# The second attention's row maxima: mask added on VectorE, a compact inverse, and values carried into the next block

## What is computed

```python
qkv = (layernorm(x) @ attn_w.T + attn_b).reshape(b, n, 16, 24).transpose(0, 2, 1, 3)
q, k, v = jnp.split(qkv, 3, axis=-1)
mask = jnp.arange(n)[:, None] <= jnp.arange(n)[None, :]
scores = jnp.where(mask, einsum('bhki,bhqi->bhkq', k, q) / sqrt(8), -10000.0)
probs = softmax(scores, axis=2)
out = einsum('bhkq,bhkl->bhql', probs, v) ...
x = x + out @ out_w.T + out_b
```

## Time and profile before

| | |
|---|---|
| median of 3 runs | 783.54 us (780.2 to 790.93) |
| profiled execution | 791.89 us, span 790.0 us, mean granted TensorE clock 0.945 |
| attention b | 343 to 601 us of the span, about |
| its first scores of block 0 | 318 to 343 us |
| PE, DVE, ACT, POOL busy | 703.7, 507.1, 454.5, 432.1 us |

### The profile page before, as it was taken

How to read it: one execution, slowest core, us unless ns; L and a number is a source line. 1 busy time by engine, 2 the same in 40 slices (tenths; PEclk the granted TensorE clock), 3 DMA queues, 4 the chain that set the end, 5 groups by cost and what they waited for, 6 DMA issues and landing times.

```text
span 790.0 us, 14471 instructions
## 1 busy us (share of the span) xinstructions
PE 703.7 (89%) x4962; PEld 490.7 (62%) x4962; DVE 507.1 (64%) x965; ACT 454.5 (58%) x801; POOL 432.1 (55%) x444
## 2 busy tenths in 40 slices
PE   4888995799999999989999889898878899999996
PEld 2455554577777776765555555555546677778784
DVE  6678884657665575566477777776566666755520
ACT  2768774465566655456456556556464455566563
POOL 4455341477778775343244444444443777777773
PEclk9999997899999999999599999999678999999998
DMA  5110410000000005504355545544102000000000
GB/s 177 38 37 19 67 19 2 1 1 0 1 0 0 1 1 187 187 2 138 133 174 176 188 147 199 176 149 135 56 27 80 1 15 14 0 13 14 14 14 27
DMA packets 30726, 51.98 MB, mean 66 GB/s; under 512 B 2256, under 2 KB 7376, under 8 KB 30672
## 3 DMA queue, kind: packets, MB, share of 16 engines
q1 hardware_dynamic: 30480, 51.01, 20.6%
q10 hardware_dynamic: 192, 0.26, 0.1%
HBM read 26.88 MB, written 24.12 MB: 65 GB/s over the span
## 4 chain that ended last, share of the span: by engine, by line
PE 49%; POOL 14%; issue 14%; DVE 11%; ACT 9%; ACTq 1%; POOLq 1%; DVEq 0%; DMA 0%
PE banks L220 45%; POOL f_h_lo L1121 5%; POOL f_g_lo L1128 5%; ACT b_prob L1439 4%; PE banks L212 2%; DVE a_mx L644 2%; POOL b_prob L1636 2%; DVE xn L182 2%; ACT a_prob L547 1%; DVE a_prob L656 1%; DVE a_straight L629 1%; ACT xn L198 1%; DVE f_hidden L1071 1%; PE banks L956 1%; DVE f_gate L1067 1%
## 5 line engine op out<-in xcount | busy, mean ns | idle before, releaser
L1128 POOL TENSOR_TENSOR f_g_lo<-f_gelu,f_g_hi 128x512 fp32r<-128x512 f32 x128 | 168.2, 1318 | 67.4 <-ACT f_g_hi L1023 67.0
L1022 ACT ACTIVATE f_gelu<-banks,cols 128x512 f32<-128x512 f32 x128 | 88.3, 690 | 140.1 <-PE banks L220 139.2
L1636 POOL TENSOR_SCALAR_AFFINE_SELECT b_prob<-b_prob 128x512 f32<-128x512 f32 x128 | 82.3, 646 | 120.2 <-ACT b_prob L1439 119.8
L220 PE MATMUL banks<-f_g_hi,whi 128*128 128x512 f32 x320 | 133.3, 416 | 15.1 <-POOL f_g_lo L1128 15.1
L1523 DVE TENSOR_REDUCE b_segment_max<-banks 128x6 f32<-128x768 f32 x128 | 115.9, 947 | 41.7 <-PE banks L220 41.7
L1439 ACT ACTIVATE b_prob<-banks 128x768 f32<-128x768 f32 x128 | 102.6, 810 | 64.9 <-PE banks L220 58.4
L220 PE MATMUL banks<-f_g_lo,whi 128*128 128x512 f32 x320 | 128.1, 400 | 0.0
L1121 POOL TENSOR_TENSOR f_h_lo<-f_hidden,f_h_hi 128x512 fp32r<-128x512 f32 x60 | 77.7, 1295 | 59.1 <-DVE f_h_hi L1074 59.1
L220 PE MATMUL banks<-f_h_hi,whi 128*128 128x512 f32 x256 | 104.4, 408 | 3.0 <-POOL f_h_lo L1121 2.5
L220 PE MATMUL banks<-f_h_lo,whi 128*128 128x512 f32 x256 | 102.1, 399 | 0.0
L1023 ACT ACTIVATE f_g_hi<-banks,cols 128x512 fp32r<-128x512 f32 x128 | 87.2, 681 | 0.0
(11 more groups left out here) (124 smaller groups left out, 1092.7 us busy)
## 6 DMA issues: line engine op xcount, KB each, us to landing
f_h_hi<-b_q_dram SPq DMA_DIRECT2D x16, 512.0 KB, 4.1
f_h_lo<-b_k_dram SPq DMA_DIRECT2D x16, 512.0 KB, 5.1
b_o_dram<-b_o SPq DMA_DIRECT2D x8, 1024.0 KB, 4.4
b_q_dram<-b_q_hi SPq DMA_DIRECT2D x16, 256.0 KB, 3.1
b_k_dram<-b_k_hi SPq DMA_DIRECT2D x16, 256.0 KB, 3.0
w_stage<-in_wF SPq DMA_DIRECT2D x8, 352.0 KB, 3.2
b_q_dram<-b_q_lo SPq DMA_DIRECT2D x8, 256.0 KB, 3.0
b_k_dram<-b_k_lo SPq DMA_DIRECT2D x8, 256.0 KB, 3.1
```

The costliest lines, as they stand in the source:

```text
L220: return nc.tensor.matmul(out, lhsT, rhs, start=start, stop=stop)
L1022: nc.scalar.activation(gf[c % 2][:, :], z_bank[c % 2], ACT.Gelu, scale=scale).then_inc(s_gf, 1)
L1128: nc.gpsimd.tensor_tensor(lo[:, c, :], gf[c % 2][:, :], hi[:, c, :].bitcast(F32), ALU.subtract).then_inc(s_glo[c % 2], 1)
L1636: nc.gpsimd.affine_select(out=pr, in_=pr, compare_op=ALU.is_ge, fill=0.0, base=0, pattern=[[0, 4], [1, P]], channel_multiplier=-1).then_in ...
```

## The change

1. `pe_first` has no mask products. Per head it makes one product of 256 columns and one of 128, and waits for all reductions of the step before.
2. `dve_first` runs, per head and query tile, one instruction that adds the mask (0 or -1e30, a zero tile for the middle third) to the scores, writes the sum as bf16 to a tile that nothing reads, and takes the maximum into the tile to be transposed. `dve_max` and its copies are gone.
3. The denominators are loaded once each as 128 x 64 and inverted by one instruction behind step 2; SP stores the inverse to DRAM and loads it repeated. POOL waits for that load.
4. The values and the output copy of step 7 move into step 0 of the next block.

```diff
 def pe_first(pe, m, n):
-                for p in range(PAIRS):
-                    wait(pe, s_red, UNITS * m.t + PAIRS * n + p - 1)
-                    for j in (2 * p, 2 * p + 1):
-                        out = first_pass[:, j, 0:3 * P].rearrange("p (c k) -> p c k", c=3)
-                        mm(out[:, 0:3:2, :], ident_b[:, :], mask[:, 0:2, :], start=True, stop=False)
-                for c, (qt, kt) in enumerate(((0, 0), (1, 0), (1, 1))):
+                wait(pe, s_red, UNITS * m.t + PAIRS * n)
+                for qt, into in ((1, slice(P, 3 * P)), (0, slice(0, P))):
                     for j in range(GROUPS):
-                        last = mm(first_pass[:, j, c * P:(c + 1) * P], q[rows_of(j), g, at + qt * P:at + (qt + 1) * P],
-                                  k[rows_of(j), g, at + kt * P:at + (kt + 1) * P], start=False, stop=c == 2)
+                        last = mm(first_pass[:, j, into], q[rows_of(j), g, at + qt * P:at + (qt + 1) * P],
+                                  k[rows_of(j), g, at:at + (qt + 1) * P])
                 last.then_inc(s_p1, 1)
...
 def dve_first(dve, m, n):
                 dve.wait_ge(s_p1, STEPS * m.t + n + 1)
+                if n % HALF == 0:
+                    wait(dve, s_mt, HALVES * (m.t - 1) + n // HALF + 1)
+                dve.sem_inc(s_turn_max, 1)
                 for p in range(PAIRS):
-                    nc.vector.reduce_max(seg[:, g, s, 2 * p:2 * p + 2, :],
-                                         first_pass[:, 2 * p:2 * p + 2, 0:3 * P].rearrange("p b (c k) -> p b c k", c=3),
-                                         AX.X).then_inc(s_red, 1)
+                    for j in (2 * p, 2 * p + 1):
+                        for qt, into in ((0, slice(0, P)), (1, slice(P, 3 * P))):
+                            last = nc.vector.tensor_tensor_reduce(
+                                out=masked[:, j, into], in0=first_pass[:, j, into], in1=mask_row[:, into], scale=1.0,
+                                scalar=MASKED, op0=ALU.add, op1=ALU.max,
+                                accum_out=mx[g // PAIRS][:, s, qt, j, g % PAIRS:g % PAIRS + 1])
+                    last.then_inc(s_red, 1)
...
-            def dve_inverse(dve, b, half):
-
-                if half == 0:
-                    dve.wait_ge(s_ol, 32 * (b.t + 1))
-                at = slice(half * T, (half + 1) * T)
-                nc.vector.reciprocal(inv[:, at], den[:, at]).then_inc(s_inv, 1)
+            def dve_inverse(dve, b):
+
+                dve.wait_ge(s_ol, 32 * (b.t + 1))
+                nc.vector.reciprocal(den_inv[:, :], den[:, :]).then_inc(s_inv, 1)
...
 pool_normalise:
-                pool.wait_ge(s_inv, HALVES * (b.t + 1))
+                pool.wait_ge(s_ol, 32 * (b.t + 1))
+                pool.wait_ge(s_il, 16 * (b.t + 1))
...
 sp_out:
-                sp.dma_start(den[:, :], view[:, DB:REP, :]).then_inc(s_ol, 16)
+                sp.dma_start(den[:, :], view[:, DB, :].rearrange("h (c t) -> h c t", t=DEN_COLS)).then_inc(s_ol, 16)
+                sp.wait_ge(s_inv, v["read"])
+                sp.dma_start(inv_dram.ap().rearrange("h (c t) -> h c t", t=DEN_COLS), den_inv[:, :]).then_inc(s_is, 16)
+                sp.wait_ge(s_is, v["stored"])
+                sp.dma_start(inv[:, :], inv_dram.ap().unsqueeze(1).to_broadcast([HB, DB, TOK])).then_inc(s_il, 16)
...
 pe_step:
                 if n:
                     pe_values(pe, b, n - 1)
+                elif before:
+                    pe_values(pe, b.after(-1), STEPS - 1)
...
 act_body:
+                    if before and n == 0:
+                        act_out(act, b.after(-1), GROUPS - 1)
...
 dve_body:
-                    if before and n in (OUT_AT - 2, OUT_AT - 1):
-                        dve_inverse(dve, b.after(-1), n - (OUT_AT - 2))
+                    if before and n == INVERSE_AT:
+                        dve_inverse(dve, b.after(-1))
```

More of the change, by code:

```diff
@@ L262, in build @@
         o_dram = nc.dram_tensor("b_o_dram", (GROUPS, P, TOK), F32)
+        inv_dram = nc.dram_tensor("b_inv_dram", (HB, TOK), F32)
         s_wB = sem("b_weights_loaded")
@@ L279, in pool_b_constants @@
                                     base=0, pattern=[[-1, P]], channel_multiplier=1).then_inc(s_cp, 1)
-            nc.gpsimd.affine_select(out=mask[:, :, :], in_=mask[:, :, :], compare_op=ALU.is_ge, fill=MASKED,
-                                    base=0, pattern=[[0, GROUPS], [-1, P]], channel_multiplier=1).then_inc(s_cp, 1)
+            nc.gpsimd.affine_select(out=mask[:, 0:3:2, :], in_=mask[:, 0:3:2, :], compare_op=ALU.is_ge, fill=MASKED,
+                                    base=0, pattern=[[0, 2], [-1, P]], channel_multiplier=1).then_inc(s_cp, 1)
         def sp_b_constants(sp):
@@ L1174, in attention_b @@
             split = {k: sb(f"b_{k}", [P, TOK], F32R) for k in ("q_hi", "q_lo", "k_hi", "k_lo")}
-            seg = sb("b_segment_max", [P, GROUPS, SEQS, GROUPS, 3])
+            masked = sb("b_masked_scores", [P, GROUPS, 3 * P], BF16)
+            mask_row = mask[:, 0:3, :].rearrange("p c k -> p (c k)")
             mx = [sb(f"b_max{i}", [P, SEQS, 2, GROUPS, PAIRS]) for i in range(HALVES)]
@@ L1179, in attention_b @@
             oT = sb("b_oT", [P, TOK])
-            den = sb("b_den", [P, TOK])
+            DEN_COLS = HB * TOK // P
+            den = sb("b_den", [P, DEN_COLS])
+            den_inv = sb("b_den_inv", [P, DEN_COLS])
             inv = sb("b_inv", [P, TOK])
@@ L1198, in attention_b @@
             s_red = sem("b_segments_reduced")
-            s_mx = sem("b_max_ready")
+            s_turn_max = sem("b_max_turn")
             s_mt = sem("b_max_transposed")
@@ L1211, in attention_b @@
             s_ol = sem("b_output_loaded")
+            s_is = sem("b_inverse_stored")
+            s_il = sem("b_inverse_loaded")
             s_on = sem("b_output_normalised")
@@ L1219, in attention_b @@
             MAX1_AT, T_AT, Q_AT, K_AT, V_AT, MAX0_AT, OUT_AT = 0, 1, 2, 3, 4, 5, 6
+            INVERSE_AT = 2
             GATE_AT = {2: 0, 4: 1, 6: 2}
@@ L1367, in pe_body @@
                     pe_step(pe, b, n, before, one, two, parts)
-                pe_values(pe, b, STEPS - 1)
+                if not one:
+                    pe_values(pe, b, STEPS - 1)
             def pe_front(pe, b, at, c):
@@ L1483, in act_body @@
                         nxt["act_tanh"](act, FIRST_BLOCK, GATE_AT[n], HEAD_PAIR)
-                act_out(act, b, GROUPS - 1)
                 if not one:
+                    act_out(act, b, GROUPS - 1)
                     nxt["act_tanh"](act, FIRST_BLOCK, KC - 1, HEAD_PAIR)
@@ L1568, in dve_body @@
                         norm.dve_apply(dve, n2, False)
-                    if one and n == MAX0_AT - 1:
-                        dve_max(dve, n1, 0)
                     if one and not two and n == OUT_AT:
@@ L1624, in dve_tail @@
                 if c == KC - 1:
-                    dve_inverse(dve, LAST_BLOCK, 0)
-                    dve_inverse(dve, LAST_BLOCK, 1)
+                    dve_inverse(dve, LAST_BLOCK)
                 if c == KC:
```

13 lines of the change are left out of this document (1 added, 12 removed).

## The result

| | before | after |
|---|---|---|
| median of 4 runs | 785.21 us (780.2 to 790.93) | 811.15 us (808.86 to 813.05) |
| profiled execution, span | 791.89, 790.0 us | 809.59, 807.6 us |
| attention b, first exponential of block 0 to that of block 7 | 223.2 us | 246.5 us |

The ratio is 1.033 (95% interval 1.025 to 1.041): slower, and outside the predicted 765 to 806. (Ratios here compare undisturbed executions only, so a median over all of a kernel's runs can lie a little above its ratio.)

A forecast was written before the change was run, and what follows sets the result against it. It took PE and ACT's exponential as a matched pair bounding the attention's half step, with PE leading overall; -12 us at equal clock and +13 from a falling clock gave +1, so 785 us, range 765 to 806.

The forecast's parts named there:

- What bounds the kernel: Attention half step with first scores: PE's issue and ACT's exponential level at about 1.45 us, so removing masks gains little.
- D = 2.2 us, reads free: VectorE's eight mask-and-maximum instructions per step take 2.2 us together, with accumulator reads hidden; the other end was 3.3.
- Rival 2: VectorE becomes the bound: D = 3.3, 804 to 806 us, chance 0.14; middle case D = 2.6, 790, chance 0.10.
- Carried values, -1.1 a block: At block turns, moving step 7's values later brings the next scores 1.6 us sooner, costing 0.5: net -1.1.
- Inverse, -1.0 + 0.5: Per block, POOL's stall for the reciprocal goes, -1.0 us; VectorE's new wait for late denominators costs PE 0.5.
- Equal clock, -1.4 a steady block: Sum for a steady attention block at unchanged clock: -0.2 + 0.4 - 1.1 - 1.0 + 0.5 = -1.4 us.
- Feed-forward, -1: Eight of 64 steps lie in the feed-forward before the attention; they gain 1 us in all.
- The clock falls in every block: Attention without 128-row mask products: granted clock well under 0.92 in blocks 0 to 6, five of eight steps low.
- The price, 0.6 us a low step: Attention step at 1.2 GHz without masks takes 4.2 us against 3.6: 21 us in all, less 8 already lost, +13.
- Rival 3: Attention clock stays down for whole blocks: +14 us, 798 to 803, chance 0.12.
- Rival 4: SP's wait for the inverse's store makes rows late for first scores: 1.5 us a block, 794, chance 0.08.
- rival C: Raised after the experiments, no chance given: PE's idle time in each step, not the rows used, lowers the clock.

The follow-up runs named there:

- e6: Kernel before with only the carried values added: 774.13 us, ratio 0.988 to before.
- e4: Kernel before with the carried values and the compact inverse, without the new maxima: 767.91 us, ratio 0.978 to before.
- e9: Changed kernel with four unused 128-row mask products per step put where PE waits for the exponential: 780.51 us, ratio 0.993 to before.
- e13: e9 with the inverse behind step 3 instead of step 2: 782.11 us, ratio 0.997 to before.
- e14: e4 with the inverse behind step 3 instead of step 2: 781.65 us, ratio 0.995 to before.
- e1: Changed kernel with the four 128-row mask products of each step issued again behind the wait for the maxima, result unused: 786.65 us, ratio 1.003 to before.
- e8: Changed kernel with the values of heads 0 and 1 moved ahead of the second pair's scores: 775.93 us, ratio 0.989 to before.
- e2: e1 with each unused mask product on 32 rows of the array instead of 128: 802.85 us, ratio 1.019 to before.
- e15: e13 with VectorE's blocks 1 to 6 written out instead of looped: 784.03 us, ratio 0.994 to before.
- e7: e1 with two unused mask products per step instead of four: 808.59 us, ratio 1.034 to before.

## Why the prediction was wrong, step by step

- **What bounds the kernel: right.** From the first exponential of a step to the second, on ScalarE, it takes 1.34 or 1.35 us at full clock in before (blocks 2 to 5) and as much in after (steps 4 to 6); at the low level 1.59 or 1.60 in after. PE waits where it issued masks:

```profile
500.67 0.45 PE L220 MATMUL banks<-f_h_hi,f_h_lo 32*128 32x256 f32 x4 [0.87 <-ACT b_prob L1445]
```

- **D = 2.2 us, reads free: right.** DVE in after (start, length), one step's first three of eight:

```profile
500.62 0.28 DVE L1536 CUSTOM_DVE_ANT_0 b_masked_scores<-banks,b_mask 128x128 bf16<-128x128 f32 x1
500.82 0.08 DVE L1536 DVE_READ_ACCUMULATOR2_ANT b_max<- 128x1 f32 x1
500.82 0.42 DVE L1536 CUSTOM_DVE_ANT_0 b_masked_scores<-banks,b_mask 128x256 bf16<-128x256 f32 x1
501.17 0.08 DVE L1536 DVE_READ_ACCUMULATOR2_ANT b_max<- 128x1 f32 x1
501.17 0.28 DVE L1536 CUSTOM_DVE_ANT_0 b_masked_scores<-banks,b_mask 128x128 bf16<-128x128 f32 x1
...
502.84 0.08 DVE L1536 DVE_READ_ACCUMULATOR2_ANT b_max<- 128x1 f32 x1
```

  0.20 to 0.21 and 0.35 us start to start, 2.22 for the eight, each read at the next one's start. Rival 2, both cases, is out, and the chosen end was the right one.
- **Carried values, -1.1 a block: right.** e6's blocks 3 to 5 take 29.3 us on average, before's three quiet ones 30.25: -1.0.
- **Inverse, -1.0 + 0.5: right in sum.** e4's blocks 3 to 5 take 28.8: -0.5. POOL's product no longer waits (510.08 in after, no releaser). The new wait for the denominators is there: in after only in block 6 (1.78 us; 2.13 in e9), where steps are short, but in e4, at full clock, in each of blocks 1 to 6, with 0.57 to 2.12 us.
- **Equal clock, -1.4 a steady block: right.** e9's blocks 2, 4 and 5 take 28.8 against 30.25: -1.4. The same blocks of e4 take 28.8 too, so in a steady block the new maxima are worth nothing, where I had +0.2.
- **Feed-forward, -1: not contradicted.** The attention starts at 342.4 against 344.7 in the profiled pair, and at 341.0 to 345.7 in the other kernels.
- **The clock falls in every block: right.** I said five of eight steps of 4.2 us in seven blocks, 147 us low. Blocks 0 to 6 of after have 2 x (1 - clock) x length = 18 + 22 + 27 + 18 + 17 + 26 + 22 = 150 us.
- **The price, 0.6 us a low step: wrong, and this is the step that failed.** Blocks 1 to 5 of after average 35.7 us with 22.1 low, against 28.9 at full clock: 6.8 / 22.1 = 0.31 us for each low one. Step by step: the 18 steps of blocks 1 to 6 of after that lie wholly at the low level take 4.83 us on average, and the same steps at full clock (e9, one of them from e4) 3.46, so each costs 1.4. The prediction had this rate on its own page (a loss of 0.33 us for each low one, from 110 products in 14 us) and used it for the time lost before; for the time after it took 5.3 - 1.08 = 4.2, as if the masks' 1.08 us at 1.2 GHz came back in full. They lie in part in the exponential's shadow at the low level too, by the argument that the prediction itself made for full clock: 0.7 comes back in the half step shown above and nothing in step 1 (4.75 us with and without). The 5.3 itself, with masks, was about right for the four wholly low steps of before (4.58 to 6.06 us, 5.36 on average); with q in it such a step is longer (6.08 in block 1 before, 5.67 after).

With the rate: blocks 0 to 6 have 150 us low against 36 (6 + 18 + 3 + 8), 115 x 0.31 = +36. My -7 and -1.7 at equal clock beside it make +27; measured +23.3. On the whole, -12 + 36 = +24 on the median, 809 for 811 measured. The 0.31 is taken from five of these seven blocks, so this sum shows that the terms fit together and tests little; with the prediction's own 0.33 it would be 38 for the 36. Rival 3, whole blocks low, is out as a mechanism, because clock 0.64 to 0.75 means half to three quarters of a block; its price was too small for the same reason. Rival 4 didn't happen in after (F never waits for a load there), but e13 and e14 show that it was a single step away.

## What to carry to other kernels

Ask of work that is to be removed what it covers and what it keeps up: where PE waits for another engine anyway, a product removed there brings nothing, and the clock can go with it, at about 0.3 us for each us spent low in this kernel, where PE makes up 49% of the chain. Look at how long PE is then idle in each step, and not only at its busy share of the whole. Use one rule for cover at both clock levels. When a change has several parts, run them apart: here two parts together brought 2.2%, and the third alone cost 4.9%.

## What the runs showed of the chip

- Filling PE's wait in each step holds the granted clock: masks on 128 rows in a line (e1 0.95), products whose result is never read (e9 0.94, 31 us faster than after), values that take twice as long (e8 0.94). Four products on 32 rows side by side, which leave the wait nearly as it is, do not (e2 0.75). Whether the rows or the idle time decide is open (rival C).
- Values of two heads take as long as those of four (0.83 for x8, 0.84 for x16), as the four heads write four groups of 32 partitions and run side by side. The Trainium skill, "TensorE: Matmul & The Clock Gate", section "Part 3: Packing small matmuls — row/col tiling", says that such tiles overlap, and the trace agrees.
- A loop's jump back can stop an engine. With the new maxima VectorE has 1821 instructions for 965, and every such kernel with the loop has one gap of 1.8 to 4.2 us at the start of block 3, where the loop of two blocks starts over (none at block 5, where it does so again); no kernel with the old reductions has it, nor e15 without the loop. Here of after:

```profile
450.10 0.08 DVE L1536 DVE_READ_ACCUMULATOR2_ANT b_max<- 128x1 f32 x1
451.98 0.87 DVE L171 BATCH_NORM_STATS2 stats<-X 128x6 f32 x4 [1.80 <-issue]
```

The Trainium skill, "Runtime: NRT & Kernel Launch", section "Instruction fetch mechanics", says that a taken branch outside the pages at hand waits for its code. The page's rows of an instruction queue (packets, MB) agree, in that more code is loaded in after:

```profile
q14 instruction: 32, 0.26, 0.1%
```

than in before:

```profile
q14 instruction: 22, 0.18, 0.1%
```

One of these packets starts at 449.9 us in after, where the gap begins, and one each within the gap or just ahead of it in e1, e7, e9 and e13 (444.2, 450.1, 437.0 and 436.0); before has none between 401 and 510 us.

- One wait can bring a fall with it. A wait of PE of 1.9 us for rows (e14, twice) or 2.1 for the maxima behind the inverse (e9, block 6) comes with 3.4 to 6.8 us at the low level, from within the wait or at most 1.5 us behind it, and the block is 3.4 to 4.4 us longer than in e4.
